# Cross-attention and gene FFN on one core: the moves of a steady tile in another order

## The reference

```
x = x + xattn(layernorm(x), ctx, pos, pos, Wq, Wkv, Wout, bout)   # x: (16, 128, 512), ctx: (16, 128, 256)
x = x + ffn(layernorm(x), Wc, temperature, genes, Wd, Wu, norm_w, scale)

xattn: q = x @ Wq; k, v = split(ctx @ Wkv); 32 heads of 16; rotations of q and k by the two positions
       w = softmax(q k^T / 4); return (w v) @ Wout + bout
ffn:   xn = rmsnorm(x) * norm_w; logits = xn @ Wc^T / temperature           # 1024 genes
       top 32 of the logits, softmax over them; expressed = weights @ genes  # 64 wide
       return tanh(expressed @ Wd^T) * xn * (expressed @ Wu^T) * scale
```

## Time and profile before

| | us |
|---|---|
| median of 3 runs (499.6 to 502.38) | 500.55 |
| profiled execution, its own time | 503.35 |
| its span | 501.4 |
| PE busy | 424.0 (85%) |
| DVE busy | 410.5 (82%) |
| POOL busy | 301.7 (60%) |
| ACT busy | 280.8 (56%) |

### The profile page before, as it was taken

How to read it: one execution, slowest core, us unless ns; L and a number is a source line. 1 busy time by engine, 2 the same in 40 slices (tenths; PEclk the granted TensorE clock), 3 DMA queues, 4 the chain that set the end, 5 groups by cost and what they waited for, 6 DMA issues and landing times.

```text
span 501.4 us, 10933 instructions
## 1 busy us (share of the span) xinstructions
PE 424.0 (85%) x3766; PEld 259.5 (52%) x3766; DVE 410.5 (82%) x677; ACT 280.8 (56%) x409; POOL 301.7 (60%) x272
## 2 busy tenths in 40 slices
PE   3756668987998999999899999999999899686985
PEld 3332445545555656565556555656565556353342
DVE  4674965498999798989998989898999897977671
ACT  3440747366665767575657574748475757452320
POOL 3011936457586778686868686868686868231430
PEclk9975898899999999999999999999999999999899
DMA  5766050614436364535354444444443644203202
GB/s 200 251 167 128 3 136 3 127 54 107 97 86 139 86 139 86 139 84 137 84 125 96 118 102 116 105 116 105 116 105 95 106 86 107 70 19 84 64 22 63
DMA packets 147920, 51.03 MB, mean 102 GB/s; under 512 B 139296, under 2 KB 141360, under 8 KB 147888
## 3 DMA queue, kind: packets, MB, share of 16 engines
q1 hardware_dynamic: 146800, 49.44, 41.6%
q10 hardware_dynamic: 1088, 1.18, 0.7%
HBM read 12.60 MB, written 4.19 MB: 33 GB/s over the span
## 4 chain that ended last, share of the span: by engine, by line
PE 43%; DVE 31%; issue 12%; DMA 6%; ACT 5%; DVEq 1%; SPq 1%; ACTq 0%; POOLq 0%
PE dense L1294 13%; DVE stage_b L1090 11%; PE gene L1294 9%; DVE top L1082 8%; PE gene L1449 5%; PE score_b L1294 4%; DVE row_max L1015 3%; DMA stage_a<-wc_raw 2%; PE dense L1417 2%; DMA stage_b<-L_xattn_Wq_dram 2%; PE score_a L1361 2%; ACT stage_b L689 2%; DVE attn L1032 2%; PE score_b L1361 1%; PE dense L1402 1%
## 5 line engine op out<-in xcount | busy, mean ns | idle before, releaser
L1082 DVE MAX8 top<-stage_b 128x8 f32<-128x1024 f32 x64 | 78.5, 1226 | 11.2 <-ACT stage_b L689 6.2
L1090 DVE MATCH_REPLACE8 stage_b<-top,stage_b 128x1024 f32<-128x1024 f32 x64 | 77.1, 1205 | 0.0
L456 POOL TENSOR_TENSOR stage_b<-stage_b,cos_t 128x512 f32<-128x512 f32 x30 | 38.2, 1274 | 58.2 <-issue 58.2
L1402 PE MATMUL dense<-stage_a,v_ext 128*32 128x128 f32 x1024 | 42.4, 286 | 8.1 <-ACT stage_a L651 7.7
L1294 PE MATMUL dense<-wq_h,xT 128*128 128x512 f16 x128 | 44.3, 408 | 1.4 <-DVE wq_l L954 1.4
L1449 PE MATMUL gene<-wcT_h,yT 128*128 128x512 f16 x128 | 45.1, 394 | 0.1
L477 POOL TENSOR_TENSOR parts<-turned,parts 128x512 f16<-128x512 f32 x30 | 34.9, 1164 | 12.3 <-issue 12.2
L1294 PE MATMUL gene<-wcT_h,yT 128*128 128x512 f16 x128 | 40.8, 380 | 0.6 <-DVE down L1129 0.6
L457 POOL TENSOR_TENSOR stage_b<-stage_b,sin_t 128x512 f32<-128x512 f32 x30 | 40.4, 1346 | 0.0
L504 POOL TENSOR_TENSOR x_ring<-x_ring,down 128x512 f32<-128x512 f32 (+1 forms) x15 | 28.1, 1876 | 19.6 <-DVE down L1129 19.6
L498 POOL TENSOR_TENSOR down<-down,yn_ring 128x512 f32<-128x512 f32 x15 | 19.4, 1293 | 33.5 <-ACT down L724 33.5
(11 more groups left out here) (175 smaller groups left out, 1121.4 us busy)
## 6 DMA issues: line engine op xcount, KB each, us to landing
out_dram<-x_ring SPq DMA_DIRECT2D x16, 256.0 KB, 2.2
x_ring<-x_dram SPq DMA_DIRECT2D x15, 256.0 KB, 2.7
ctx_sb<-ctx_dram SPq DMA_DIRECT2D x16, 128.0 KB, 2.1
wc_raw<-L_ffn_Wc_dram SPq DMA_DIRECT2D x4, 512.0 KB, 6.1
stage_b<-L_xattn_Wq_dram ACTq DMA_DIRECT2D x4, 256.0 KB, 5.7
stage_a<-L_xattn_Wkv_dram SPq DMA_DIRECT2D x2, 512.0 KB, 8.4
stage_a<-L_xattn_Wout_dram SPq DMA_DIRECT2D x1, 1024.0 KB, 8.7
qT<-neg_maxT SPq DMA_DIRECT2D x32, 8.0 KB
```

Of the source, the lines that this page charges most:

```text
L456: pool.tensor_tensor(halves(qk_cos), halves(qk_sb), trig(cos_t, t), ALU.mult).then_inc(s_cosm[n], 1)
L1082: nc.vector.max(top[:, 8 * n:8 * n + 8], logit if n == 0 else rest).then_inc(s_top[n], 1)
L1090: nc.vector.match_replace(rest, top[:, 8 * n:8 * n + 8], logit if n == 0 else rest, REMOVED).then_inc(s_rem[n], 1)
L1402: last = nc.tensor.matmul(dense[rows, at:at + P], v_ext[:, head], probs[g % 2][:, slot_at:slot_at + P], start=True, stop=True)
```

## The change

Six moves, no operation added or removed:

- SP: `turn_w` of a tile is issued at the end of a pass, before `store` and `next_x`, instead of at the start of the next pass.
- ACT: both `read_oT` stand before k's `split_hi`; `norm1_apply` stands behind `attn_hi`.
- DVE: `norm1_shift` goes from between `negate_top` and the last `remove_top` to behind `normalise` (and the early weights' low parts).
- DVE: `group_max` of group 0 stands before `residual`.
- PE: `project_out` is cut in two halves of 6 matmuls, with `scores` of group 0 between them.
- PE: `values` 3 stands before `down_up` 0, and `transpose_o` before `down_up` 1.

```diff
@@ SP, iteration
-                if t7 is not None:
-                    turn_w(t7)
                 if t4 is not None:
                     shift(t4, 0)
                     shift(t4, 1)
@@
                 if later(t1, 1):
                     next_ctx(t1)
+                if t6 is not None:
+                    turn_w(t6)
                 if t7 is not None:
                     store(t7)
@@ ACT, iteration
                     exp_group(t3, 3)
+                if t3 is not None:
+                    read_oT(t3, 0)
+                    read_oT(t3, 1)
                 if later(t2):
                     split_hi(t2, 1)
-                if t3 is not None:
-                    read_oT(t3, 0)
-                    read_oT(t3, 1)
@@
-                if later(t1):
-                    norm1_apply(t1)
                 if t3 is not None:
                     attn_hi(t3)
@@
                 if later(t1):
+                    norm1_apply(t1)
                     x_hi(t1)
@@ DVE, iteration
                     negate_top(t6)
-                if later(t2, 1):
-                    norm1_shift(t2)
                 if t6 is not None:
                     remove_top(t6, 3)
@@
                     job_lo(3)
+                if later(t2, 1):
+                    norm1_shift(t2)
                 if later(t1, 1):
                     norm1_stats(t1)
@@
                     mask(t6)
+                if t3 is not None:
+                    group_max(t3, 0)
                 if t4 is not None:
                     residual(t4)
@@
                 if t3 is not None:
-                    group_max(t3, 0)
                     group_max(t3, 1)
@@ PE
-            def project_out(t):
-                pe.wait_ge(s_aT_h, t + 1)
-                pe.wait_ge(s_aT_l, t + 1)
-                if first(t):
-                    pe.wait_ge(s_split_out, 1)
-                three_pass(dense[:, 512:1024], psum_parts(aT_h, aT_l), (columns(wout_h, 0), columns(wout_l, 0)),
-                           XK).then_inc(s_proj, 1)
+            def project_out(t, half):
+                if half == 0:
+                    pe.wait_ge(s_aT_h, t + 1)
+                    pe.wait_ge(s_aT_l, t + 1)
+                    if first(t):
+                        pe.wait_ge(s_split_out, 1)
+                (ah, al), (wh, wl) = psum_parts(aT_h, aT_l), (columns(wout_h, 0), columns(wout_l, 0))
+                for k in (2 * half, 2 * half + 1):
+                    for n, (lhs, rhs) in enumerate(((ah, wh), (ah, wl), (al, wh))):
+                        last = nc.tensor.matmul(dense[:, 512:1024], lhs(k), rhs(k), start=(k == 0 and n == 0),
+                                                stop=(k == XK - 1 and n == 2))
+                if half == 1:
+                    last.then_inc(s_proj, 1)
@@ PE, iteration
                 if t4 is not None:
-                    project_out(t4)
+                    project_out(t4, 0)
+                if t3 is not None:
+                    scores(t3, 0)
+                if t4 is not None:
+                    project_out(t4, 1)
@@
                 if t3 is not None:
-                    scores(t3, 0)
                     scores(t3, 1)
@@
-                if t6 is not None:
-                    down_up(t6, 0)
                 if t3 is not None:
                     values(t3, 3)
@@
                 if t6 is not None:
+                    down_up(t6, 0)
+                if t3 is not None:
+                    transpose_o(t3)
+                if t6 is not None:
                     down_up(t6, 1)
-                if t3 is not None:
-                    transpose_o(t3)
```

More of the change, by code:

```diff
@@ L736, in iteration @@
                     exp_group(t3, 3)
-                if later(t2):
-                    split_hi(t2, 1)
                 if t3 is not None:
@@ L741, in iteration @@
                     read_oT(t3, 1)
+                if later(t2):
+                    split_hi(t2, 1)
                 if first(t3):
@@ L1571, in iteration @@
                 if t6 is not None:
-                    down_up(t6, 1)
+                    down_up(t6, 0)
                 if t3 is not None:
                     transpose_o(t3)
+                if t6 is not None:
+                    down_up(t6, 1)
                 if first(t3):
```

## The result

| | before | after |
|---|---|---|
| median of 4 runs (lowest to highest) | 501.47 (499.6 to 502.62) | 515.08 (513.14 to 518.77) |
| profiled execution, its own time | 503.35 | 518.77 |
| its span | 501.4 | 516.2 |

The ratio is 1.0273, with a 95% interval of 1.0231 to 1.0315: slower by 13.6 us. The forecast was 506.5 with a range up to 511. Its direction came true and its size did not. The two profiled spans differ by 14.8, where the sum had +5.9 for them.

The account below looks back on a forecast made before the run. Two rings bound the kernel, the one through DVE's top search tighter; the change makes q's transfer due. 13 × 0.50 − 0.6 = +5.9 takes the profiled 503.35 to 509.3, the median to 506.5; range 497.0 to 511.0.

Parts of the forecast that it names:

- The ring through q's transfer: Exponentials, oT reads, k and q copies, SP's turns, scores, logits1, ctx, maxima; 1.57 us slack at q's landing before.
- 13 × 0.50: Loss term of the sum: cT_l and the next tile 0.50 us later (0.71 − 0.21), in 13 passes.
- Part 4: PE, project_out in halves: scores wait about 1.2 us for q's transfer, logits1 starts 0.71 later.
- 13 times: Count of full-pattern passes, 6 to 17 and once more at scores of pass 18, each priced as the steady tile.
- Part 5: SP, turn_w before store and next_x: queue allows 0.2 to 0.7 us delay, leaves the 0.50; saves 0.6 once.
- The one-off wait of 0.56: PE's wait for the weights' late transfer at the rolled loop's start; forecast to vanish, saving 0.6 us.
- Part 1: DVE, norm1_shift behind normalise: attn could be ready 1.05 us earlier; cost in the new place taken as nothing.
- the lock: DVE two-SBUF-input and POOL SBUF instructions exclude each other; as rival, norm1_shift ends 1.1 us late again, 497.7, 4%.
- Part 3: ACT, oT read before k's high copy: k's high part 1.48 us later, q's 0.41 later.
- The transfer is no limit: Rival: qT lands before about 298.67, PE gains 0.47 us a tile, time 493.9; 19%.
- It cancels: Rival: q lands between 299.3 and 299.5, cT_l stays where it was, 500 to 501.5 us; 17%.
- SP's variant: Rival: SP's queue sets the pace as well, +0.7 us a tile, 509.8; within the forecast's 60%.

Follow-up runs that it names:

- u_split: Changed kernel with project_out whole again, both halves before scores of group 0: 499.13 us, ratio 0.9959 to before.
- u_act: Changed kernel with k's high copy back in front of the two reads of oT on ACT: 505.48 us, ratio 1.0095 to before.
- u_w: Changed kernel with turn_w back at the start of the next pass, before the shift: 518.42 us, ratio 1.0357 to before.
- u_shift: Changed kernel with norm1_shift back between negate_top and the last remove_top: 514.50 us, ratio 1.0271 to before.
- b_shift: Changed kernel with project_out whole before scores and norm1_shift back in its old place: 499.41 us, ratio 0.9963 to before.
- o_act: Kernel before with only both reads of oT moved in front of k's high copy on ACT: 506.09 us, ratio 1.0095 to before.
- u_both: Changed kernel with k's high copy back before the reads of oT and project_out whole before scores: 502.09 us, ratio 1.0006 to before.

## Why the prediction was right in kind and wrong in size

**What held.** The ring through q's transfer became the bound, and u_split and u_act show it from both sides. Most signs that the prediction named are in the trace: the hole before values 3, the turn of attn at PE's pace, turns 1.57 apart (1.6 to 1.7 forecast), q's landing 5.56 behind kT's issue (5.64), the wait in front of cT_l, and normalise 2.54 behind the last MAX8 (2.5). The residual kept a wait of 0.52 beside the new one, and the tile takes 26.06, not 25.85. The wait for qT itself is 0.76 here, not 1.2, since project_out first waits 0.45 for aT_l; that costs nothing, as the transfer ends last either way.

The step that failed is the term 13 × 0.50 of the sum, in both factors. It stood at 6.5; on the two profiled spans the thirteen stretches cost 12.4 + 2.9 = 15.3.

**Part 4, the 0.50: the PE work behind the wait, and what it delays.** "Logits1 starts 2.12 after scores0" was measured as 2.26: the second half takes 1.60 instead of 1.48, with a first matmul of 0.50, and the two handovers around it 0.33 each. Logits1 is so 0.85 later against the ring and not 0.71. The 0.21 that DVE's cT_l had to spare leaves 0.64. By SP's queue it is the same: 0.85 less the 0.22 that ctx-load-to-shift got shorter, 4.36 to 4.14, is 0.63. The steady period measured +0.63. The averages agree: behind the end of the last exponential, over passes 9 to 14, scores of group 0 start 9.47 later, just as forecast (299.85 − 290.38), and logits1 11.72 later, not 9.47 + 2.12 = 11.59. The term was 0.14 too small.

Of the two paths the forecast took the wrong one. It priced cT_l and the maxima, but in the steady tile the maxima are ready 0.38 before SP comes to the shift. A delay of theirs of 0.50 alone would have moved the shift by some 0.12 (an estimate from these two numbers). The delay is carried by transpose_ctx, ctx's load and the rest of SP's queue, as u_w shows from the other side.

**"13 times", the larger error.** The sum priced every pass as the steady tile that I had read. Only six periods are that. At the loop's edges a slow transfer meets PE with no slack: q's turn holds SP's queue for 3.17 at pass 8 and lands 5.1 after its issue, at pass 16 it lands 5.46 after, and PE waits 2.01 and 2.40. In the profiled execution of before q's turns of these two passes landed after 3.6 and 3.8; the 5.1 of the earlier trace rows is k's of pass 9. In that of u_split both are slow, 5.1 and 5.2, but the whole project_out covers most of it: PE waits 0.57 and 1.25, and the two periods lose 0.38 and 0.76 against before, not 1.71 and 2.13. Behind the wait at pass 16 PE's granted clock falls to 0.65 and 0.50, and the 12 matmuls of logits1 take 3.45 instead of 2.69. U_shift shows that pass 8's wait comes again and pass 16's does not, so some 3 us of this account belong to the one execution and not to the kernel. The account of the 8.9 that the sum was short, on the spans: 0.8 in the steady periods, 5.6 in the six others (8.6 − 6 × 0.50), 0.6 for the saving below, 2.4 behind scores of pass 18 (2.9 − 0.50), less the 0.5 by which the changed kernel leads at pass 6.

**Part 5, turn_w.** "This queue does not change the 0.50" failed: the queue is the tight path of a steady tile, and turn_w's shorter issue in front of the other issues (1.67) is why the change cost 13.6 and not about 17 (u_w). The one-off wait of 0.56, which stands in PE's pass 7, is gone, but nothing is saved by it, because scores of pass 8 wait for qT instead.

**Part 1, norm1_shift.** Its sign came true (normalise 2.54 behind the last MAX8), for a reason that I had not seen. The prediction had the move save 1.05 and pay it again only if it met the lock. It does meet it: 1.15 in the new place, beside POOL's copy of q (300.73 and 300.71). The Trainium skill ("SBUF — State Buffer", Who interferes with whom) says that such a pair of instructions excludes each other, whoever starts first, and the trace agrees: 1.15 or 0.15 for the same 128x1 instruction. But the 1.14 of before was gone already by Part 3: once the reads of oT stand in front of k's copy, POOL's copy of k starts after norm1_shift in its old place, which then takes 0.15 (u_shift, b_shift, o_act). I priced each move against the old neighbours of the other.

**Part 3, k's late copy.** Its cost through qT was right. That the gate's delay is covered in the changed kernel was right too: the same wait stands in u_split, which is faster than before; that it would cost 4.6 in the kernel before (o_act) was named as a possibility only. What was missing is its gain, 2.4 to 3.0 us in the changed kernel with project_out whole.

**The rivals.** "The transfer is no limit" fell with the wait in all 16 tiles. "It cancels" fell too; u_both is where the parts cancel, at 502.09. The lock was met again, and hidden by the wait for qT, as the prediction said of that case. SP's variant, +0.7 a tile and 509.8, was the nearest, in path and in size.

**Open.** Why q's transfer is slow at pass 8, and in some executions at pass 16, was not tried, nor how much of the 2.9 behind pass 18 is PE's clock (granted 0.85 in the 22.25 us behind scores of pass 18, 0.92 before) and how much is waiting. The profiled execution of after is also 3.7 above its median, that of before 1.9, so the account above is one of spans and some 1.2 larger than the medians'. The new places of values 3 and transpose_o, of norm1_apply and of group_max 0 were never undone alone.

## What to carry to other kernels

Before a consumer is moved up, compare its new time with the landing of its transfer, and count as delayed everything that stands behind it in its in-order queue: here six matmuls behind a wait cost 16 us. Parts of a change that meet in one ring are to be priced together, since alone they gave +4.6 and +6.8 and together +24.4, and one of them even changed sign with PE's order. Follow every path to the point where they meet, here SP's shift, before one of them is priced. And read the first and last passes of a loop before multiplying a steady tile: half of this loss was there, part of it in one execution and not in the next, so a second trace of a kernel of the same time is worth taking.

## What the runs showed of the hardware

- A DVE instruction on 128x1 took 0.15 us alone and 1.15 beside a POOL operation of 1.16, in either place. With POOL's operation starting 0.66 after it, as in u_shift, nothing of this was left: the median of its 16 is 0.153, against 1.132 before.
- The same DMA turn of 128 partitions is not one price: q's held the queue for 1.76 to 2.30 us in passes 10 to 15 and for 3.17 at pass 8, and the landings of all 32 after lie between 3.7 and 5.7.
- PE waited 2.40 us at pass 16 at a granted clock of 1.00. Then, though busy throughout, it was granted 0.65 in the first 2 us, 0.50 (1.2 GHz) in the next and 0.99 in the third. The 512-wide f16 matmuls of logits1 start up to 0.43 apart in it, and 0.22 apart in the steady tile. That a wait brings this on is not shown: u_w waited 1.82 at pass 8 and fell to 0.69 and 0.50 behind it, u_shift waited 2.89 there and stayed at 1.00.
